# Causal masks and output scaling moved to VectorE, rotary products spread over three steps, in a transformer layer on eight cores

## The chip, the cores and the metric

The kernel runs on the 8 cores of one Trainium2 chip, one batch row each, with no exchange between them. The metric is device time in microseconds (us) of the slowest core. Engines are named as in the profile: PE is TensorE, DVE VectorE, ACT ScalarE, POOL GpSimd, and SP issues most transfers.

## The reference

One layer: a layer norm, causal attention with rotary positions in 16 heads of 64, and a feed-forward block with dequantized weights whose SiLU multiplies the attention output.

```python
xn = _layernorm(x)
q, k = rope(xn @ Wq), rope(xn @ Wk); v = xn @ Wv
attn = softmax(where(causal, q @ k.T / 8, -inf)); s = (attn @ v) @ Wo
h = layernorm(xn)
y = silu(h @ dequant(fc1) + b1); z = y @ dequant(fc2) + b2
x = x + s * silu(xn + 0.5 * z)
```

Each core has 2048 rows of 1024; the feed-forward width is 4096.

## The kernel before, in words

The program is written out in Python as one list of instructions for each engine; each engine works through its list in order, and semaphores hold it where it needs another's result. A core goes through four stages.

1. Rows are normalized and transposed, the first head pair is projected, and a quarter of the values (to about 112 us).
2. Attention. Heads are taken in pairs, `m` = 0 to 7. A pair has four groups of 512 queries, `qg`, and a group 2 `qg` + 2 steps `c` of two key tiles (128 keys each), so 20 steps for a pair and 160 in all. A step has the two tiles' `scores` (4 matmuls into `ps[0]` and `ps[1]`, then ACT's exponential to one of six buffers `pbuf`), filler matmuls, and then the `values` of the step before (8 matmuls that add into `ps[2]`: the weighted values in its first bank, the sum of weights in its second). Fillers are the projections of later pairs (`unit`, 8 matmuls, 8 units of work) and of the values (`v_unit`). They stand in one list and are handed out in proportion by `fill_to`, some 3.7 units of a matmul each in a middle step and 8.4 in a group's second, until step 133. From there, in the last part of pair 6 and pair 7, there are none ("the last head" below). A filler unit fills one of the two banks of `ps[3]`; DVE copies it out (L337 for queries and keys, L376 for values), and the unit after next waits for that copy (`f_free`).
3. `fc1`, 1024 matmuls with SiLU on ACT (620 to 850 us).
4. `fc2` and the output projection (850 us to the end).

What else stands in the attention steps: once a pair's queries or keys (`j` = 0, 1) are complete, SP issues four transfers that swap rows (`swp<-raw`), and three steps later `rope` has DVE multiply `swp` by the sine, `raw` by the cosine, and add both, each over 2048 columns. `later(n, fn)` puts work off by n steps, `step()` runs what is due. The sum is held back until the first step of the pair before, since it overwrites what the pair before that one read. 64 jobs (`dq_load`, `dq_do`) dequantize weights on DVE and write them to memory, 0.42 a step. On the two diagonal steps of each group (`c` = 2 `qg` and 2 `qg` + 1) the exponentials of a tile are multiplied by a mask (128 x 2 x 128) on POOL. At a group's end ACT takes logarithm and exponential of the weight sums (`linv`), DVE copies the weighted values out of their bank (`sol`), and POOL multiplies the two into `o_fm`. In the last head DVE also scales the activations for the next stage (`make_h`).

## Time and profile before

| | |
|---|---|
| median of 3 runs | 1144.39 us (1143.58 to 1147.31) |
| the profiled execution's own time | 1140.83 us |
| its span, slowest core (core 2) | 1139.3 us |
| spans of the other cores | 1124.7 to 1138.8 us |
| PE busy | 975.2 us (86%) |
| ACT busy | 475.6 us (42%) |
| DVE busy | 421.2 us (37%) |
| POOL busy | 181.2 us (16%) |
| PE's share of the chain that ended last | 70% |

A busy share is a mean over stages with different limits, so the stages are read apart. An engine's idle time is put down to what it waited for last; idle time of an engine that is not the limit costs nothing. The granted clock is TensorE's, as a share of 2.4 GHz.

### The profile page before, as it was taken

Reading aid. Unit: us, or ns where it says so; the run is one execution under the profiler, and the core shown is the slowest. Engines: PE = TensorE matmul, PEld = TensorE weight load, DVE = VectorE, ACT = ScalarE, POOL = GpSimd, SP = SyncE. Lnnn points to the kernel's source line nnn. Section 1 sums busy time; section 2 is a strip of 40 time slices with the busy share of each in tenths; the row PEclk is TensorE's granted clock in tenths of the full one; section 3 lists DMA queues with packets and bytes.
Section 4 is the critical chain, followed back from the end, with each engine's and each line's share of the span. In section 5 each row is a group of like instructions: output and inputs, shape, how many; then the busy total and the mean of one; then the engine's idle time right before and its main releaser. Section 6 shows DMA issues by size and latency. Waiting matters only on the chain.

```text
span 1139.3 us, 15271 instructions; the slowest of 8 cores (1124.7 to 1139.3 us)
## 1 busy us (share of the span) xinstructions
PE 975.2 (86%) x5465; PEld 423.5 (37%) x5465; DVE 421.2 (37%) x516; ACT 475.6 (42%) x616; POOL 181.2 (16%) x202
## 2 busy tenths in 40 slices
PE   3654588888788978799767999999997999999998
PEld 2332332332234322353223344444443444444443
DVE  3562454655564474546554000000002333333233
ACT  2232265656666765587888333333330000000000
POOL 1001031414243341425254000000000000000000
PEclk9767898989999998999889999999998999999999
DMA  7256457656586666457763855555547432234121
GB/s 186 75 169 102 102 187 237 174 196 195 158 248 201 206 187 203 158 186 245 239 184 100 184 152 157 154 155 157 150 111 267 139 139 83 112 139 144 50 65 37
DMA packets 92745, 180.47 MB, mean 158 GB/s; under 512 B 8048, under 2 KB 45056, under 8 KB 91392
## 3 DMA queue, kind: packets, MB, share of 16 engines
q1 hardware_dynamic: 84624, 170.52, 47.3%
q0 software_dynamic: 8048, 8.98, 5.5%
q8 instruction: 46, 0.75, 0.3%
q14 instruction: 27, 0.22, 0.1%
HBM read 138.11 MB, written 41.95 MB: 158 GB/s over the span
## 4 chain that ended last, share of the span: by engine, by line
PE 70%; DMA 8%; DVE 8%; issue 6%; ACT 5%; POOL 1%; SPq 1%; DVEq 0%; ACTq 0%; POOLq 0%
PE ps L860 20%; PE ps L793 18%; PE ps L328 8%; PE ps L664 8%; PE ps L367 5%; PE ps L625 5%; PE ps L835 4%; ACT pb L639 3%; DMA swp<-raw 3%; DMA y_spill<-yst 2%; DMA xbuf<-x 2%; DVE raw L337 1%; DVE raw L444 1%; POOL pb L645 1%; DVE swp L443 1%
## 5 line engine op out<-in xcount | busy, mean ns | idle before, releaser
L639 ACT ACTIVATE pb<-ps,negub 128x1024 bf16<-128x1024 f32 (+1 forms) x320 | 296.3, 981 | 148.4 <-PE ps L625 147.8
L793 PE MATMUL ps<-xn,w1t 128*128 128x512 bf16 x1024 | 224.0, 382 | 2.6 <-ACT yst L804 2.6
L328 PE MATMUL ps<-xn,wqk 128*128 128x512 bf16 x512 | 143.2, 404 | 40.0 <-DVE raw L337 33.9
L645 POOL TENSOR_TENSOR pb<-pb,msk 128x256 bf16<-128x256 bf16 x128 | 116.8, 928 | 266.3 <-ACT pb L639 263.8
L793 PEld LDWEIGHTS ps<-xn,w1t 128*128 128x128 bf16 x1024 | 100.7, 98 | 125.5 <-issue 8.3
L804 ACT ACTIVATE yst<-ps,b 128x512 bf16<-128x512 f32 x128 | 87.5, 687 | 136.3 <-PE ps L793 128.2
L875 ACT ACTIVATE tf<-tf 128x512 f32<-128x512 f32 x32 | 20.1, 630 | 267.3 <-DVE tf L871 267.3
L860 PE MATMUL ps<-w2a,ybuf 128*128 128x512 bf16 x512 | 118.3, 385 | 6.7 <-DMA ybuf<-y_spill 6.7
L860 PE MATMUL ps<-w2b,ybuf 128*128 128x512 bf16 x512 | 115.7, 379 | 0.0
L625 PE MATMUL ps<-qk,qk 64*128 64x512 bf16 (+3 forms) x640 | 101.4, 367 | 12.3 <-ACT pb L639 11.3
L664 PE MATMUL ps<-pb,v_tm 128*64 128x512 bf16 (+3 forms) x640 | 98.3, 378 | 13.7 <-POOL pb L645 11.7
L367 PE MATMUL ps<-wv,xn 128*128 128x256 bf16 x512 | 74.6, 295 | 41.2 <-DVE v_tm L376 29.1
L852 DVE TENSOR_SCALAR tf<-xt,mv,r 128x1024 f32<-128x1024 f32 x16 | 12.9, 809 | 241.5 <-DMA xt<-x 241.5
L664 PE MATMUL ps<-pb,ones 128*64 128x512 bf16 (+3 forms) x640 | 91.7, 367 | 0.0
L601 DVE SCALAR_TENSOR_TENSOR dqo<-dqi,dqs 128x1024 bf16<-128x1024 int32 x64 | 86.3, 1348 | 7.0 <-DMA dqs<-fc_scales 6.8
L328 PEld LDWEIGHTS ps<-xn,wqk 128*128 128x128 bf16 x512 | 43.0, 101 | 113.6 <-issue 84.4
L337 DVE CAST raw<-ps 128x512 bf16<-128x512 f32 x64 | 43.9, 688 | 111.1 <-PE ps L328 110.9
L860 PEld LDWEIGHTS ps<-w2a,ybuf 128*128 128x128 bf16 x512 | 50.6, 99 | 69.2 <-issue 10.5
L871 DVE SCALAR_TENSOR_TENSOR tf<-ps,tf 128x512 f32<-128x512 f32 x32 | 22.1, 691 | 145.0 <-PE ps L860 145.0
L367 PEld LDWEIGHTS ps<-wv,xn 128*128 128x128 bf16 x512 | 49.7, 105 | 66.9 <-issue 58.4
L860 PEld LDWEIGHTS ps<-w2b,ybuf 128*128 128x128 bf16 x512 | 50.1, 98 | 60.4
L625 PEld LDWEIGHTS ps<-qk,qk 64*128 64x128 bf16 x640 | 27.8, 94 | 87.7 <-issue 81.1
(74 smaller groups left out, 603.7 us busy)
## 6 DMA issues: line engine op xcount, KB each, us to landing
dqi<-fc_q SPq DMA_DIRECT2D x64, 512.0 KB, 4.7
dqs<-fc_scales SPq DMA_DIRECT2D x64, 512.0 KB, 6.1
w_deq<-dqo SPq DMA_DIRECT2D x64, 256.0 KB, 2.5
y_spill<-yst SPq DMA_DIRECT2D x32, 512.0 KB, 3.7
ybuf<-y_spill SPq DMA_DIRECT2D x8, 2048.0 KB, 10.0
xbuf<-x SPq DMA_DIRECT2D x16, 512.0 KB, 5.2
swp<-raw SPq DMA_DIRECT2D x64, 128.0 KB, 5.0
w1t<-w_deq SPq DMA_DIRECT2D x32, 256.0 KB, 4.2
```

The source lines that it names most:

```text
L328: fn = (lambda e: e.matmul(p, w[:, 128 * fc:128 * (fc + 1)], xn[:, S * fc + 512 * tg:S * fc + 512 * (tg + 1)], start=(fc == 0), stop=(fc = ...
L337: t_raw[(m, j, tg)] = VE.tick(lambda e: e.tensor_copy(raw[j][:, 512 * tg:512 * (tg + 1)], p))
L367: fn = (lambda e: e.matmul(z[:, 256 * u:256 * (u + 1)], xn[:, S * fc + 128 * t:S * fc + 128 * (t + 1)], wv[p][:, 256 * fc:256 * (fc + 1)], ...
L601: t_dv[k] = VE.tick(lambda e: e.scalar_tensor_tensor(dqo[k % 2][:], dqi[k % 2][:], -128.0, dqs[k % 2][:], ALU.add, ALU.mult))
L625: fn = (lambda jj, r: lambda e: e.matmul(z[:, 512 * jj + off:512 * (jj + 1)], ka[r:r + 64, 128 * kt:128 * (kt + 1)], qa[r:r + 64, 512 * qg ...
L639: tok = SC.tick(lambda e: e.activation(fap(p, [[512, 2], [1, n]], offset=off), fap(z, [[512, 2], [1, n]], offset=off), AF.Exp, bias=negub[ ...
L645: tok = GP.tick(lambda e: e.tensor_mul(fap(p, [[512, 2], [1, 128]], offset=off), fap(p, [[512, 2], [1, 128]], offset=off), fap(msk, [[0, 2 ...
L664: fn = (lambda what, jj, kt, p, off, w: lambda e: e.matmul(ps[2][64 * jj:64 * (jj + 1), 512 * what + off:512 * (what + 1)], w, p[:, 512 * ...
L793: fn = (lambda k, fc, f, tg: lambda e: e.matmul(ring[k], w1t[f % 4][:, 128 * fc:128 * (fc + 1)], xn[:, S * fc + 512 * tg:S * fc + 512 * (t ...
L804: t_ring[k] = SC.tick((lambda k, f, tg: lambda e: e.activation(yst[f % 2][:, 512 * tg:512 * (tg + 1)], ring[k], AF.Silu, bias=b1[:, f:f + ...
L835: fn = (lambda hf, fc: lambda e: e.matmul(z[:, 512 * hf:512 * (hf + 1)], o_fm[:, S * fc + 128 * t:S * fc + 128 * (t + 1)], wo[:, 1024 * fc ...
L860: fn = (lambda f, wt, lo, hi: lambda e: e.matmul(z[:, lo:hi], ybuf[i][:, 256 * f + 128 * (t % 2):256 * f + 128 * (t % 2) + 128], wt[:, 102 ...
```

## The change

Four things are moved, and none is computed in another way.

- The masks are multiplied on DVE instead of POOL, at the start of the next step (`mask`).
- The weighted values are multiplied by `linv` on DVE straight from their PSUM bank (`scale`), at the start of the next step; the copy to `sol` and POOL's product are gone.
- When a new group begins (`c` == 0), the values of the last step of the group before stand ahead of the fillers, not behind them.
- `rope` has its first product three steps after the unit, as before, the second a step later, and the sum a step after that, or at the first step of the pair before. In a step where such work is due no dequantization is written, unless more than two are owed; these are caught up afterwards. Ahead of the first step six calls of `step()` take the place of three.

```diff
@@ -157,8 +157,7 @@
     swp = [at(f"swp{j}", S, BF16, RE + 8192 + 4096 * j) for j in range(2)]
     sq = at("sq", S, BF16, RE + 16384)
     pbuf = [at(f"pb{i}", 1024, BF16, RF + 2048 * i) for i in range(6)]
-    sol = [at(f"sol{i}", 512, F32, RG + 2048 * i) for i in range(2)]
-    linv = [at(f"linv{i}", 512, F32, RG + 4096 + 2048 * i) for i in range(2)]
+    linv = [at(f"linv{i}", 512, F32, RG + 2048 * i) for i in range(2)]
     wqk = [[at(f"wqk{i}{j}", 1024, BF16, RH + 4096 * i + 2048 * j) for j in range(2)] for i in range(2)]
     cos_t = at("cos_t", S, BF16, RI)
     sin_t = at("sin_t", S, BF16, RI + 4096)
@@ -439,19 +439,22 @@
             f_free[b] = t_neg[m]
 
         def rope(m, j):
-            VE.wait(t_swap[(m, j)], t_cos)
-            VE.do(lambda e: e.tensor_mul(swp[j][:], swp[j][:], sin_t[:]))
-            tok = VE.tick(lambda e: e.tensor_mul(raw[j][:], raw[j][:], cos_t[:]))
-
-            def add():
+
+            def by_sin():
+                VE.wait(t_swap[(m, j)], t_cos)
+                VE.do(lambda e: e.tensor_mul(swp[j][:], swp[j][:], sin_t[:]))
+
+            def by_cos():
+                tok = VE.tick(lambda e: e.tensor_mul(raw[j][:], raw[j][:], cos_t[:]))
+
+                later(max(1, 7 + 20 * (m - 1) - now[0]), lambda: add(tok))
+
+            def add(tok):
                 VE.wait(tok, t_last_s.get(m - 2))
                 t_rope[(m, j)] = VE.tick(lambda e: e.tensor_add(qb[m % 2][j][:], raw[j][:], swp[j][:]))
 
-
-            if now[0] >= 4 + 20 * (m - 1):
-                add()
-            else:
-                later(4 + 20 * (m - 1) - now[0], add)
+            by_sin()
+            later(1, by_cos)
 
 
         for t in range(1, 4):
@@ -573,8 +576,8 @@
 
         total = sum(c for c, _ in fill)
         lead = 33.0
-        fill_to(12.0)
-        for _ in range(3):
+        fill_to(15.0)
+        for _ in range(6):
             step()
         fill_to(lead)
 
@@ -640,12 +644,16 @@
                 fap(p, [[512, 2], [1, n]], offset=off), fap(z, [[512, 2], [1, n]], offset=off),
                 AF.Exp, bias=negub[:, m:m + 1], scale=0.125))
             t_exp_bank[half] = tok
-            if kt >= 4 * qg:
-                GP.wait(tok, t_msk)
-                tok = GP.tick(lambda e: e.tensor_mul(
-                    fap(p, [[512, 2], [1, 128]], offset=off), fap(p, [[512, 2], [1, 128]], offset=off),
-                    fap(msk, [[0, 2], [1, 128]])))
             t_p[(m, qg, kt)] = tok
+
+        def mask(m, qg, kt):
+
+            off = 128 * (kt - 4 * qg)
+            p = pbuf[slot_of[(m, qg, kt)]]
+            VE.wait(t_p[(m, qg, kt)], t_msk)
+            t_p[(m, qg, kt)] = VE.tick(lambda e: e.tensor_mul(
+                fap(p, [[512, 2], [1, 128]], offset=off), fap(p, [[512, 2], [1, 128]], offset=off),
+                fap(msk, [[0, 2], [1, 128]])))
 
         def values(m, qg, c):
 
@@ -682,13 +690,16 @@
             t_bank[1] = SC.tick(lambda e: e.activation(linv[i][:], ps[2][:, 512:1024], AF.Ln))
             SC.wait(t_bank[1])
             t_li = SC.tick(lambda e: e.activation(linv[i][:], linv[i][:], AF.Exp, scale=-1.0))
-            VE.wait(tok, t_o.get(g - 2))
-            t_bank[0] = VE.tick(lambda e: e.tensor_copy(sol[i][:], ps[2][:, 0:512]))
-            GP.wait(t_li, t_bank[0])
-            if m >= 4:
-                GP.wait(t_vmm[m - 4])
-            t_o[g] = GP.tick(lambda e: e.tensor_mul(
-                o_fm[:, S * m + 512 * qg:S * m + 512 * (qg + 1)], sol[i][:], linv[i][:]))
+
+            def scale():
+                VE.wait(t_li)
+                if m >= 4:
+                    VE.wait(t_vmm[m - 4])
+                t_o[g] = VE.tick(lambda e: e.tensor_mul(
+                    o_fm[:, S * m + 512 * qg:S * m + 512 * (qg + 1)], ps[2][:, 0:512], linv[i][:]))
+                t_bank[0] = t_o[g]
+
+            at_next.append(scale)
 
 
         kinds = []
@@ -732,19 +743,27 @@
         prev = None
         ns = len(kinds)
         for s, (m, qg, c, w) in enumerate(kinds):
-            step()
+            ran = step()
+            for fn in at_next:
+                fn()
+            at_next.clear()
+            if prev and prev[2] >= 2 * prev[1]:
+                for kt in (2 * prev[2], 2 * prev[2] + 1):
+                    mask(prev[0], prev[1], kt)
             for kt in (2 * c, 2 * c + 1):
                 scores(m, qg, kt)
+            if c == 0 and prev:
+                values(*prev)
             if s < last_fill:
                 run += w
                 fill_to(lead + (total - lead) * run / weight)
             else:
                 fill_to(1e9)
-            if prev:
+            if c > 0:
                 values(*prev)
             prev = (m, qg, c)
             want = min(len(jobs), (len(jobs) * (s + 1)) // (ns - 8))
-            while done < want:
+            while done < want and (not ran or want - done > 2):
                 dq_do(done)
                 if done + 2 < len(jobs):
                     dq_load(done + 2)
@@ -757,7 +776,16 @@
                 for f in range(3):
                     load_w1(f)
         step()
+        for kt in (2 * prev[2], 2 * prev[2] + 1):
+            mask(prev[0], prev[1], kt)
         values(*prev)
+        for fn in at_next:
+            fn()
+        while done < len(jobs):
+            dq_do(done)
+            if done + 2 < len(jobs):
+                dq_load(done + 2)
+            done += 1
         t_att = (PE.sem, PE.n)
         while put_off:
             step()
```

How this moves instructions is seen at two places. The first is on DVE in the middle of pair 1, where the keys of pair 2 (`raw_73`, `swp_75`) get their rotary products while the second quarter of the values is projected (L376 copies a finished filler unit). Before:

```order
L418 TENSOR_REDUCE nm_62<-ps 1x2
L422 TENSOR_SCALAR nm_62<-nm_62 1x1
L430 TENSOR_SCALAR stb<-nm_62 1x1
L601 SCALAR_TENSOR_TENSOR dqo_98<-dqi_94,dqs_96 128x1024
L443 TENSOR_TENSOR swp_75<-swp_75,sin_t 128x2048
L444 TENSOR_TENSOR raw_73<-raw_73,cos_t 128x2048
L448 TENSOR_TENSOR qk_69<-raw_73,swp_75 128x2048
L376 CAST v_tm<-ps 128x2x256
L438 COPY negub<-ps 128x1
L601 SCALAR_TENSOR_TENSOR dqo_97<-dqi_93,dqs_95 128x1024
```

Now (DVE's rotary lines are L445, L448 and L454 here, and the dequantization is L604):

```order
L418 TENSOR_REDUCE nm_62<-ps 1x2
L422 TENSOR_SCALAR nm_62<-nm_62 1x1
L430 TENSOR_SCALAR stb<-nm_62 1x1
L604 SCALAR_TENSOR_TENSOR dqo_96<-dqi_92,dqs_94 128x1024
L445 TENSOR_TENSOR swp_75<-swp_75,sin_t 128x2048
L376 CAST v_tm<-ps 128x2x256
L448 TENSOR_TENSOR raw_73<-raw_73,cos_t 128x2048
L438 COPY negub<-ps 128x1
L454 TENSOR_TENSOR qk_69<-raw_73,swp_75 128x2048
L654 TENSOR_TENSOR pb_77<-pb_77,msk 128x2x128
L654 TENSOR_TENSOR pb_78<-pb_78,msk 128x2x128
```

The copy of the filler unit stood behind all three rotary operations and now stands behind the first; the second and the sum follow it, and two masks (L654) stand behind the sum.

The second place is on PE where pair 2 begins after the last group of pair 1. L625 (L629 now) is scores, L328 filler, L664 (L672 now) values, with `v_tm` for the weighted values and `ones` for the sums. Before:

```order
L664 MATMUL ps<-pb_81,ones_50 64x512 x2
L664 MATMUL ps<-pb_82,ones_50 64x384 x2
L625 MATMUL ps<-qk_68,qk_69 128x512 x2
L625 MATMUL ps<-qk_68,qk_69 128x384 x2
L328 MATMUL ps<-xn,wqk_89 128x512 x4
L328 MATMUL ps<-xn,wqk_90 128x512
L664 MATMUL ps<-pb_77,v_tm 64x256 x2
L664 MATMUL ps<-pb_78,v_tm 64x128 x2
L664 MATMUL ps<-pb_77,ones_50 64x256 x2
```

Now:

```order
L672 MATMUL ps<-pb_81,ones_50 64x512 x2
L672 MATMUL ps<-pb_82,ones_50 64x384 x2
L629 MATMUL ps<-qk_68,qk_69 128x512 x2
L629 MATMUL ps<-qk_68,qk_69 128x384 x2
L672 MATMUL ps<-pb_77,v_tm 64x256 x2
L672 MATMUL ps<-pb_78,v_tm 64x128 x2
L672 MATMUL ps<-pb_77,ones_50 64x256 x2
L672 MATMUL ps<-pb_78,ones_50 64x128 x2
L328 MATMUL ps<-xn,wqk_87 128x512 x4
```

The values of the finished group (`pb_77`, `pb_78`) stood behind the new group's scores and five filler matmuls; they now come right behind the scores.

## Rows read from the trace of the kernel before

**Rows 1.** Stretches, core 2: busy us of PE, PEld, DVE, ACT, POOL; clock, DMA, GB/s.

```profile
112.00:130.00 18.00, 7.26 (x47) 4.67 (x43) 10.08 (x14) 1.78 (x3) 0.00 (x0) 0.70 0.46 58
130.00:545.00 415.00, 354.11 (x2399) 138.59 (x2399) 222.82 (x249) 271.25 (x323) 135.91 (x140) 0.95 0.64 197
545.00:620.00 75.00, 54.34 (x379) 19.06 (x379) 40.13 (x39) 62.10 (x74) 30.76 (x30) 0.91 0.61 188
620.00:850.00 230.00, 226.29 (x1040) 101.86 (x1041) 0.69 (x1) 90.02 (x131) 5.59 (x10) 0.99 0.56 150
```

**Rows 2.** PE's waits while fillers last, 130 to 545 us: us, times, longest.

```profile
PE ps L328 <- DVE raw L337: 33.9, 17, 4.9
PE ps L367 <- DVE v_tm L376: 18.6, 8, 5.3
PE ps L664 <- POOL pb L645: 4.2, 9, 1.2
PE ps L625 <- ACT pb L639: 1.3, 4, 0.6
PE ps L328 <- DVE v_tm L376: 1.1, 1, 1.1
```

**Rows 3.** PE's waits in the last head, 545 to 620 us.

```profile
PE ps L664 <- POOL pb L645: 7.1, 10, 1.2
```

**Rows 4.** PE's timeline, nine of its long waits: start, us, [idle before, releaser].

```profile
163.90 0.59 PE L328 MATMUL ps<-xn,wqk 128*128 128x512 bf16 x1 [2.23 <-DVE raw L337]
...
185.69 1.86 PE L328 MATMUL ps<-xn,wqk 128*128 128x512 bf16 x4 [4.12 <-DVE raw L337]
...
233.24 1.01 PE L367 MATMUL ps<-wv,xn 128*128 128x256 bf16 x4 [5.28 <-DVE v_tm L376]
...
279.15 0.38 PE L328 MATMUL ps<-xn,wqk 128*128 128x512 bf16 x1 [3.16 <-DVE raw L337]
...
299.25 0.38 PE L328 MATMUL ps<-xn,wqk 128*128 128x512 bf16 x1 [4.01 <-DVE raw L337]
...
426.57 1.00 PE L328 MATMUL ps<-xn,wqk 128*128 128x512 bf16 x2 [3.17 <-DVE raw L337]
...
446.79 0.38 PE L328 MATMUL ps<-xn,wqk 128*128 128x512 bf16 x1 [4.86 <-DVE raw L337]
...
476.91 0.60 PE L367 MATMUL ps<-wv,xn 128*128 128x256 bf16 x4 [3.98 <-DVE v_tm L376]
...
529.40 0.81 PE L328 MATMUL ps<-xn,wqk 128*128 128x512 bf16 x3 [1.06 <-DVE raw L337]
```

**Rows 5.** DVE's timeline behind the wait that ends at 233.24 us.

```profile
227.66 1.23 DVE L601 SCALAR_TENSOR_TENSOR dqo<-dqi,dqs 128x1024 bf16<-128x1024 int32 x1
228.81 1.22 DVE L443 TENSOR_TENSOR swp<-swp,sin_t 128x2048 bf16<-128x2048 bf16 x1
229.94 1.22 DVE L444 TENSOR_TENSOR raw<-raw,cos_t 128x2048 bf16<-128x2048 bf16 x1
231.26 1.23 DVE L448 TENSOR_TENSOR qk<-raw,swp 128x2048 bf16<-128x2048 bf16 x1
232.41 0.69 DVE L376 CAST v_tm<-ps 128x512 bf16<-128x512 f32 x1
```

**Rows 6.** One stretch around that wait, columns as in rows 1.

```profile
232.10:238.90 6.80, 5.66 (x25) 2.06 (x25) 1.74 (x4) 1.91 (x2) 0.67 (x1) 0.50 0.27 92
```

**Rows 7.** Groups by line, whole span: count, busy us, mean ns, idle before.

```profile
L645 POOL TENSOR_TENSOR pb<-pb,msk 128x256 bf16<-128x256 bf16 x128 | 116.8, 928 | 266.3 <-ACT pb L639 263.8
...
L601 DVE SCALAR_TENSOR_TENSOR dqo<-dqi,dqs 128x1024 bf16<-128x1024 int32 x64 | 86.3, 1348 | 7.0 <-DMA dqs<-fc_scales 6.8
...
L686 DVE COPY sol<-ps 128x512 f32<-128x512 f32 x32 | 22.0, 688 | 44.4 <-PE ps L664 41.5 <-PE ps L625 1.5 <-POOL pb L645 1.2
...
L504 DVE TENSOR_TENSOR g2t<-g2t,mv 128x16 f32<-128x16 f32 x1 | 0.2, 175 | 0.1
```

**Rows 8.** DVE's waits for the swap transfer, 112 to 618 us.

```profile
DVE swp L443 <- DMA swp<-raw: 14.0, 5, 5.3
```

More of the change, by code:

```diff
@@ L229, in step @@
                 p[1]()
+            return len(due)
         t_c = None
@@ L608, in build_nc @@
         t_bank = [None, None]
+        at_next = []
         t_o = {}
```

## The prediction

> **What bounds the kernel now.** I read the profile in this order. First the table of stretches [rows 1]. The last two stages, from 620 us on, are untouched by the change, and TensorE (PE) is all but full there (226 of 230 us in the first of them). In the attention stage PE is busy for 354 of 415 us while filler matmuls last (130 to 545 us) and for 54 of 75 us in the last head, where there are none. ScalarE (ACT) is busy 271 of 415 us and 62 of 75 us. So with fillers PE sets the pace and ACT is starved by it; in the last head ACT is near its limit.
>
> Then PE's waits [rows 2]. With fillers PE loses 33.9 + 18.6 + 1.1 = 53.6 us to DVE's copies out of the two filler banks (L337, L376), 4.2 us to masks on POOL, 1.3 us to ACT. In the last head it loses 7.1 us to masks [rows 3]. Then PE's long waits in order of time [rows 4]. Of the 26 waits for those copies 15 take 1.06 us or more: the row at 163.90 is the first, that at 529.40 the last. Seven are longer than 2.46 us: 4.12, 5.28, 3.16, 4.01, 3.17, 4.86 and 3.98, together 28.6 us. The other eight (2.23, 2.08, 1.68, 1.86, 2.26, 1.40, 1.67, 1.06) make 14.2 us, the fifteen 42.8. The other eleven are the wait for a copy that has just begun.
>
> What is late is seen on DVE in one of them [rows 5]. PE wants the bank at 227.96. DVE, which works in the order of its program, has a dequantization (from 227.66), the three rotary operations (228.81, 229.94, 231.26) and only then the copy (232.41). From the first product's end to the copy there are 232.41 − 229.94 = 2.47 us, which the second product and the sum fill; so it is in the other windows too.
>
> After such a wait PE is slow: in the 6.8 us around that one the granted clock is 0.50, the lower level of 1.2 GHz [rows 6]. Over the 415 us it is 0.95 [rows 1], so 2 × 0.05 × 415 = 41 us ran at the lower level and cost half, 20 us. These 41 us lie in ten spans, each beside one of the waits of 1.86 us or more, 11 in all; the one of 2.08 us has none.
>
> **The change part by part.**
>
> *Rotary products over three steps.* Nothing is removed; the second product comes a step after the first, the sum a step after that or later, and a filler copy that is written between goes ahead of them. That is what the first pair of listings shows, at this very wait: the copy passes two of three operations. The wait there would be 5.28 − 2.46 = 2.8 us. Taking 2.46 us from each of the fifteen leaves 28.6 − 7 × 2.46 = 11.4 us in the seven long ones and nothing in the eight, a gain of 42.8 − 11.4 = 31.4 us. Not every one will find its copy between two pieces, and the shortest waits keep the length of their own copy (0.69 us [rows 5]), so I take 28 us. The bounds are 53.6 us (every wait for DVE goes) and 0 (the copy always lands outside the split).
> The dequantizations are held out of the steps that run a rotary piece; before, seven steps held a whole rotary group and one of 1.23 us. That is inside these 28 us. They are caught up two at a time in nine steps, 2.5 us in one piece. With the two banks, PE stops for that only where a copy is due within it.
> At the start (112 to 130 us) all six rotary pieces still stand in one piece without a filler between them: PE has 7.3 us busy in those 18 us [rows 1], and I count nothing there. Six steps in place of three move nothing on the engines by themselves.
>
> *The clock.* Of eleven waits of 1.86 us or more, two are left by the sum above (2.8 and 2.4 us). I leave three to be safe: 8 of 11 of the 20 us is 14.5, and I take 13 us. Bounds: 0 and 20.
>
> *Masks from POOL to DVE, a step later.* 128 operations of 928 ns leave POOL [rows 7]. What PE waits for them is 4.2 us with fillers and 7.1 us in the last head [rows 2, 3], 11.3 in all; I take 9 us. On DVE no row shows this form. The nearest are a two-input product of bfloat16, 2048 elements in 1.22 us [rows 5], and one of 16 float32 elements in 0.175 us [rows 7]. Between them lies 0.51 ns an element, so 0.175 + 256 × 0.51 = 0.31 us; at the float32 price (0.69 us for 512 elements [rows 7], 1.04 ns) it is 0.44 us. I take 0.31, the nearest row being the one of the same type: 104 masks in 415 us are 32 us of DVE. Against this DVE gets time back from POOL: a dequantization takes 1348 ns in the mean and 1.23 us where POOL is quiet [rows 5, 7], some 7 us over the 64, and the rotary products gain too. DVE's 223 us of 415 would become some 240, and it is not the bound.
> The row shows operations of DVE stretched when POOL runs. The Trainium skill ("SBUF — State Buffer", "SBUF: two separate sides") says why: VectorE with two SBUF inputs and GpSimd take one pair of ports in turns, and the loser is blocked for the whole instruction. By it a blocked operation would wait for a POOL mask's full 0.93 us, and the gain here would be some 7 us of DVE time either way; the sum does not change.
>
> *What the masks add to DVE's queue.* This is the price. A mask stands behind the copies and the dequantization of the step before, and PE's value products wait for it. For the first diagonal step of a group, from the timeline: values come some 0.8 us after the exponentials of that step end, masks need 0.6 us, so a copy and a dequantization just ahead make PE wait some 0.8 us. A filler unit ends in that step 0.44 of the time and 0.42 dequantizations fall on a step: 26 groups × 0.18 × 0.8 = 4 us. For the last step, whose values now stand ahead of the fillers, 26 × 0.11 × 1.1 = 3 us. A rotary piece of 1.22 us stands ahead in some 3 of 10 of these 52 steps and costs half a us: 8 us. Sum 15 us, of which I take 14. Bounds: 0 (PE always later), and 26 × 1.5 = 39 us if every group end waits for a piece of work and the masks. In the last head DVE also scales the activations for the next stage there, two operations of 1.22 and 0.97 us every second step, but PE has slack against ACT.
>
> *Values scaled from their bank.* The copy of 688 ns and POOL's product of some 1.4 us become one product from PSUM, by the nearest row 688 ns [rows 7]: nothing added. The accumulator's first bank is now free after ACT's two operations and this product, some 1.4 us later than by the copy. With fillers the next group's values stand behind a step's scores and 8.4 units of filler; that covers it. Without fillers the wait is 1 us, four times, beside ACT, which is the limit there: nothing. The second pair of listings shows the last values of a group ahead of the fillers. ACT takes the exponentials of the new group first in either order, so its logarithm starts when it did, and I count nothing for the move.
>
> **Sum.** −28 − 13 − 9 + 14 = −36 us. The profiled execution took 1140.8 us, and so 1104.8; the median shown, 1144.4, is 3.6 us above it, so I forecast 1108.
>
> **The rivals.**
> *More goes than I count.* If PE's waits for DVE fall to the 10.8 us of the eleven short ones, the clock stays up (−20) and the masks cost 5 us: −42.8 − 20 − 11.3 + 5 = −69 against 1144.4, and with a few left over some 1084. For it: DVE is free for 190 of 415 us. Against: three of the long waits also hold a wait for the swap transfer.
> *The waits only move.* The first product still waits three steps after the transfer is issued; DVE stood idle 14.0 us for it, five times, up to 5.3 us [rows 8]. Where it does, copies, masks and the scaling now all stand behind. If the masks' price is half as much again for that (+21) and the rotary term and the clock's give half (−14 − 7, with −9 for POOL), the sum is −9, so 1135.
> *No change* within 0.3%, about 3.4 us, which is what a measurement of this kernel can tell: the same, with the gain and price equal.
> *Slower.* DVE becomes the serial hub: every group's values wait for exponential, DVE's queue and mask. If each of the 32 group ends and of the 32 steps before it waited 1.5 us where none was before, that is 96 us; the gain of 50 us is used up at 0.8 us each, and at 1 us the time is 1144 + 64 − 50 = 1158. The rows speak against it: masks need two short operations, and DVE is idle for nearly half of the stage. The Trainium skill ("TensorE: Matmul & The Clock Gate", "Architectural detail") calls VectorE's queue strictly first in, first out, and so does the order in [rows 5]; that is what this rival needs.
> *The change doesn't do what it says* is excluded: the listings show it.
>
> **How the numbers follow.** Forecast (own range 1092 to 1122): 0.60. More: 0.14. Waits only move: 0.12. No change: 0.05. Slower: 0.09. Faster by over 0.3% is 0.60 + 0.14 + 0.12 = 0.86. The range for 8 in 10 leaves out the slow case, no change and half of "more": 1082 to 1136.
>
> **What would show it.** Right: PE's waits for L337 and L376 between start and last filler fall from 53.6 to some 25 us, the clock there rises to 0.98, waits for POOL are gone, DVE's masks take some 0.3 us, the stage up to 620 us ends some 36 us sooner, and the stages behind keep their length. Wrong: value products (L672) that wait for masks by more than 20 us in all; swap waits on DVE well over 14 us; long waits for L337 that keep their 4 to 5 us.

## The result: slower, where faster was forecast

The changed kernel takes 1156.09 us (median of 6 runs), the kernel before, run beside it, 1144.28 us (6 runs). The ratio is 1.0078, with a 95% interval of 1.004 to 1.0115. In two of the six runs of the changed kernel (1218.12 and 1289.81 us) one half of the chip had a lower granted clock; the median holds them, the ratio leaves them out. Forecast were 1108 us and a range of 1082 to 1136. The profiled run took 1154.38 us, its span is 1152.8 us, on core 1. The first matmul of the stage behind attention starts at 634.19 us; before it started at 620.50 us. What follows it lasts 518.6 us, before 518.8 us. So all that is lost is lost by the end of attention.

Here are the same stretches of the changed kernel as in [rows 1], with the same columns (busy us of PE, PEld, DVE, ACT and POOL, then clock, DMA share and GB/s):

```profile
112.00:130.00 18.00, 6.94 (x45) 4.53 (x44) 9.76 (x13) 1.78 (x3) 0.00 (x0) 0.72 0.38 48
130.00:545.00 415.00, 348.13 (x2348) 135.71 (x2345) 223.97 (x346) 264.09 (x315) 5.38 (x10) 0.94 0.64 193
545.00:620.00 75.00, 51.42 (x348) 18.50 (x349) 42.41 (x62) 57.72 (x70) 0.53 (x1) 0.84 0.71 209
```

PE does 6 us less in the 415 us than before and 3 us less in the 75 us, at a lower clock in both. POOL is all but empty, and DVE's sum is what it was (224 against 223 us): it took the masks in, its dequantizations are shorter (1219 ns in the mean, 1348 before), and less of its other work falls into these 415 us, since everything is later.

The next view holds the waits of the changed kernel between 112 and 640 us (us in total, times, longest), those of PE for DVE and those of DVE for transfers (six rows of the view; those of PE for ACT and of DVE for other engines are left out):

```profile
DVE dqo L604 <- DMA dqs<-fc_scales: 43.3, 15, 7.4
PE ps L328 <- DVE raw L337: 30.9, 14, 7.7
PE ps L672 <- DVE pb L654: 27.1, 22, 4.7
PE ps L367 <- DVE v_tm L376: 24.1, 10, 9.2
DVE swp L445 <- DMA swp<-raw: 15.1, 4, 5.5
PE ps L672 <- DVE o_fm L698: 6.6, 4, 1.7
```

The first row was not in the forecast. Before, DVE waited 6.8 us, three times, for the scales of a dequantization; now it waits 43.3 us, fifteen times. The copies of the filler units (L337, L376) are waited for nearly as long as before, with a longest wait of 7.7 us where [rows 2] have 4.9 (the 9.2 us row lies ahead of 130 us; before it was 9.6). The waits for masks are 27.1 us, where POOL's were 11.7.

DVE's timeline of the changed kernel shows one of the fifteen (start, us, operation, in brackets the idle time before it and its releaser):

```profile
438.53 2.35 DVE L604 SCALAR_TENSOR_TENSOR dqo<-dqi,dqs 128x1024 bf16<-128x1024 int32 x2
447.79 1.23 DVE L604 SCALAR_TENSOR_TENSOR dqo<-dqi,dqs 128x1024 bf16<-128x1024 int32 x1 [6.91 <-DMA dqs<-fc_scales]
448.93 0.68 DVE L408 TENSOR_REDUCE nm<-ps 128x1 f32<-128x512 f32 x1
449.53 1.21 DVE L445 TENSOR_TENSOR swp<-swp,sin_t 128x2048 bf16<-128x2048 bf16 x1
450.67 0.68 DVE L337 CAST raw<-ps 128x512 bf16<-128x512 f32 x1
```

and SP's, of the same place, when the loads were sent:

```profile
440.38 0.45 SPq L60 DMA_DIRECT2D dqi<-fc_q  x1
440.88 0.45 SPq L60 DMA_DIRECT2D dqs<-fc_scales  x1
...
441.92 0.43 SPq L60 DMA_DIRECT2D dqi<-fc_q  x1
442.39 0.93 SPq L60 DMA_DIRECT2D dqs<-fc_scales  x1
```

and PE's:

```profile
451.49 1.44 PE L328 MATMUL ps<-xn,wqk 128*128 128x512 bf16 x3 [7.69 <-DVE raw L337]
```

This reads as follows. Dequantizations held back during the rotary steps are caught up two in one piece at 438.53; this happens ten times in the changed kernel and never in the one before. A pair empties both input buffers. Each load goes out behind the dequantization that freed its buffer, the first at 440.38 and 440.88 (codes and scales), the second at 441.92 and 442.39; the next dequantization stands ready in DVE's queue and waits 6.9 us for the first of them. Behind it stand the reduction, the rotary product and, at 450.67, the copy that PE needs: PE stands for 7.7 us. The load is not an unusual one: it takes about the median from issue to landing, 6.9 us for scales (6.1 us before). What was lost is mostly the start ahead of time.

In the last head, where masks and scaling stand behind such a wait, it reads so (DVE, same columns):

```profile
563.45 2.47 DVE L604 SCALAR_TENSOR_TENSOR dqo<-dqi,dqs 128x1024 bf16<-128x1024 int32 x2
573.31 1.23 DVE L604 SCALAR_TENSOR_TENSOR dqo<-dqi,dqs 128x1024 bf16<-128x1024 int32 x1 [7.39 <-DMA dqs<-fc_scales]
576.52 1.23 DVE L604 SCALAR_TENSOR_TENSOR dqo<-dqi,dqs 128x1024 bf16<-128x1024 int32 x1 [1.98 <-DMA dqs<-fc_scales]
577.66 1.00 DVE L654 TENSOR_TENSOR pb<-pb,msk 128x256 bf16<-128x256 bf16 x4
584.38 1.22 DVE L604 SCALAR_TENSOR_TENSOR dqo<-dqi,dqs 128x1024 bf16<-128x1024 int32 x1 [5.72 <-DMA dqs<-fc_scales]
585.52 0.68 DVE L698 TENSOR_TENSOR o_fm<-ps,linv 128x512 bf16<-128x512 f32 x1
586.13 0.89 DVE L654 TENSOR_TENSOR pb<-pb,msk 128x256 bf16<-128x256 bf16 x4
```

One pair has three waits behind it, 15.1 us in all. The scaling and the masks at 585.52 and 586.13 came right behind the last, and PE waited 4.7 us for those masks, with no filler to do.

### The profile page after: what moved, and what is told of

It is laid out like the page before. It is cut to its first block, busy times and chain, and to the rows that moved or that the text cites. A ratio compares the mean times of both kernels' runs of the same rounds, so it can differ in the third digit from the quotient of the medians.

```text
span 1152.8 us, 15075 instructions; the slowest of 8 cores (1128.3 to 1152.8 us)
## 1 busy us (share of the span) xinstructions
PE 976.0 (85%) x5465; PEld 423.8 (37%) x5465; DVE 429.5 (37%) x644; ACT 475.8 (41%) x616; POOL 19.1 (2%) x42
## 2 busy tenths in 40 slices
DMA packets 92744, 180.47 MB, mean 157 GB/s; under 512 B 8048, under 2 KB 45056, under 8 KB 91392
## 4 chain that ended last, share of the span: by engine, by line
PE 70%; DMA 10%; DVE 8%; issue 6%; ACT 5%; SPq 1%; DVEq 0%; ACTq 0%; POOL 0%; POOLq 0%
PE ps L888 19%; PE ps L821 18%; PE ps L672 9%; PE ps L328 9%; PE ps L367 5%; PE ps L629 5%; PE ps L863 4%; DMA dqs<-fc_scales 4%; ACT pb L643 2%; DMA y_spill<-yst 2%; DVE dqo L604 1%; DMA xbuf<-x 1%; DVE raw L337 1%; DMA swp<-raw 1%; DMA wv<-wv 1%
## 5 line engine op out<-in xcount | busy, mean ns | idle before, releaser
L328 PE MATMUL ps<-xn,wqk 128*128 128x512 bf16 x512 | 143.6, 406 | 37.1 <-DVE raw L337 30.9
L903 ACT ACTIVATE tf<-tf 128x512 f32<-128x512 f32 x32 | 20.1, 629 | 267.5 <-DVE tf L899 267.5
L672 PE MATMUL ps<-pb,v_tm 128*64 128x512 bf16 (+3 forms) x640 | 97.7, 381 | 34.1 <-DVE pb L654 27.1
L629 PE MATMUL ps<-qk,qk 64*128 64x512 bf16 (+3 forms) x640 | 101.4, 372 | 11.9 <-ACT pb L643 10.8
L672 PE MATMUL ps<-pb,ones 128*64 128x512 bf16 (+3 forms) x640 | 93.5, 372 | 0.0
L604 DVE SCALAR_TENSOR_TENSOR dqo<-dqi,dqs 128x1024 bf16<-128x1024 int32 x64 | 77.2, 1219 | 43.4 <-DMA dqs<-fc_scales 43.3
L328 PEld LDWEIGHTS ps<-xn,wqk 128*128 128x128 bf16 x512 | 43.4, 101 | 107.4 <-issue 76.3
L337 DVE CAST raw<-ps 128x512 bf16<-128x512 f32 x64 | 44.1, 689 | 93.6 <-PE ps L328 93.5
L672 PEld LDWEIGHTS ps<-pb,v_tm 128*64 128x64 bf16 x640 | 27.9, 111 | 96.3 <-issue 94.3
L629 PEld LDWEIGHTS ps<-qk,qk 64*128 64x128 bf16 x640 | 26.1, 95 | 90.5 <-issue 88.0
```

Source lines behind the costliest of these rows:

```text
L328: fn = (lambda e: e.matmul(p, w[:, 128 * fc:128 * (fc + 1)], xn[:, S * fc + 512 * tg:S * fc + 512 * (tg + 1)], start=(fc == 0), stop=(fc = ...
L337: t_raw[(m, j, tg)] = VE.tick(lambda e: e.tensor_copy(raw[j][:, 512 * tg:512 * (tg + 1)], p))
L604: t_dv[k] = VE.tick(lambda e: e.scalar_tensor_tensor(dqo[k % 2][:], dqi[k % 2][:], -128.0, dqs[k % 2][:], ALU.add, ALU.mult))
L629: fn = (lambda jj, r: lambda e: e.matmul(z[:, 512 * jj + off:512 * (jj + 1)], ka[r:r + 64, 128 * kt:128 * (kt + 1)], qa[r:r + 64, 512 * qg ...
L672: fn = (lambda what, jj, kt, p, off, w: lambda e: e.matmul(ps[2][64 * jj:64 * (jj + 1), 512 * what + off:512 * (what + 1)], w, p[:, 512 * ...
```

## The experiments

The theory (H) from these rows: the holding back of dequantizations ("the hold" below), to which the prediction gave no price of its own, is what turns the gain into a loss, by way of the input buffers. Its rivals: the masks and the scaling on DVE cost it (M), the last values ahead of the fillers cost it (V), or the split of the rotary products gives nothing (R). Each run has the ratio of its time to that of the kernel before on the same chip, with its 95% interval.

**Without the hold.** The changed kernel, each step with its due dequantizations:

```diff
-            while done < want and (not ran or want - done > 2):
+            while done < want:
```

> The changed kernel with its dequantizations written where they were before, also in steps that run rotary work. Theory H (holding them back is the fault: two are then done at once, both buffers are loaded in one round, and DVE stands before the next one): DVE's waits for the loads fall from 43.3 us to under 12, PE's waits for masks from 27.1 us to under 15, its waits for filler copies from 56 to under 45, and the time to 1120 to 1135 us. Theory M (the masks and the scaling in DVE's queue are the fault, whatever the loads do): PE's waits for masks stay above 20 us and the time stays at 1145 to 1158 us.

Measured: 1130.64 us, ratio 0.9878 (0.9859 to 0.9898). That is 2.0% less than with the hold, and faster than before. Its waits between 112 and 640 us:

```profile
PE ps L672 <- DVE pb L654: 22.2, 22, 2.0
PE ps L367 <- DVE v_tm L376: 21.6, 9, 9.2
PE ps L328 <- DVE raw L337: 21.3, 15, 5.6
DVE swp L445 <- DMA swp<-raw: 10.1, 6, 5.0
DVE dqo L604 <- DMA dqs<-fc_scales: 9.1, 2, 6.9
PE ps L672 <- DVE o_fm L698: 6.3, 4, 1.6
```

Time, waits for scales (43.3 to 9.1 us) and waits for copies are as H expects; PE's for L337 fall from 30.9 to 21.3. The waits for masks miss it: 22.2 us, where H expected under 15. They have another cause.

**The hold alone**, put into the kernel before, whose rotary group stays whole (`step()` also returns how many pieces it ran, as in the changed kernel, and what is owed at the end is caught up there):

```diff
-            step()
+            ran = step()
...
-            while done < want:
+            while done < want and (not ran or want - done > 2):
```

> The kernel before with one part of the change: dequantizations are held out of steps with rotary work and caught up later; masks, scaling, rotary products and values as before. Theory H: DVE's waits for the loads rise from 6.8 us to over 20, and the time is 1148 to 1158 us. Theory M: the loads' waits are covered or small, and the time is 1138 to 1147 us.

Measured: 1144.56 us, ratio 0.9996 (0.9976 to 1.0015). That is M's range; H expected 1148 to 1158 us, and this expectation failed, though the waits for scales rise as it said, to 20.1 us, nine times, against 6.8 before. The traces show a difference to the changed kernel: here no two dequantizations stand in one piece, where the changed kernel has ten such pairs, and only 7.7 of the 20.1 us fall between 130 and 545 us, where fillers last (25.5 of 43.3 in the changed kernel). So the hold costs by what it meets in the changed kernel.

**A third pair of input buffers** in the changed kernel, hold and all; a load then goes out three dequantizations ahead (the third load at the start and the semaphore slots that go with it are left out here):

```diff
-    dqi = [at(f"dqi{i}", 1024, I32, RK + 4096 * i) for i in range(2)]
-    dqs = [at(f"dqs{i}", 1024, F32, RK + 8192 + 4096 * i) for i in range(2)]
+    dqi = [at(f"dqi{i}", 1024, I32, RK + 4096 * i if i < 2 else RG + 4096) for i in range(3)]
+    dqs = [at(f"dqs{i}", 1024, F32, RK + 8192 + 4096 * i if i < 2 else RG + 8192) for i in range(3)]
...
-                if done + 2 < len(jobs):
-                    dq_load(done + 2)
+                if done + 3 < len(jobs):
+                    dq_load(done + 3)
```

> The changed kernel, dequantizations held back as it does, but with three pairs of input buffers for them, so that a load is issued three jobs ahead and not two. Theory H: DVE's waits for the loads fall from 43.3 us to under 10, and the time to 1120 to 1135 us, as in the run without holding back. If it is not the loads but the double dequantization itself (2.4 us in one piece) that costs: the loads' waits fall, but the time stays above 1145 us. Theory M: 1145 to 1158 us too, with PE's waits for masks above 20 us.

Measured: 1133.63 us, ratio 0.9897 (0.9876 to 0.9918). Here the hold stays and only the loads are early, and the time is that without the hold (the intervals overlap). No wait for scales is left; one for the store of a dequantized tile takes its place (w_deq, 10.8 us, five times). The ten pairs are still there. So the hold's price goes through the empty input buffers, and no price of the 2.5 us that a pair takes is seen beyond the intervals (the two ratios are 0.2% apart).

**The split alone**, in the kernel before: `rope` as in the change's diff, and six calls of `step()` ahead of the first step.

```diff
-            VE.wait(t_swap[(m, j)], t_cos)
-            VE.do(lambda e: e.tensor_mul(swp[j][:], swp[j][:], sin_t[:]))
-            tok = VE.tick(lambda e: e.tensor_mul(raw[j][:], raw[j][:], cos_t[:]))
...
+            by_sin()
+            later(1, by_cos)
...
-        for _ in range(3):
+        for _ in range(6):
             step()
```

> The kernel before with one part of the change: the rotary products over three steps; dequantizations where they were. The prediction's step (2.46 us off each long wait): PE's waits for filler copies between 130 and 545 us fall from 53.6 to 25 to 32 us, the time to 1105 to 1118 us. The rival that the waits only move: they fall by less than 12 us and the time stays above 1134 us.

Measured: 1123.5 us, ratio 0.9801 (0.9782 to 0.982). R falls: the split gives 2.0%, some 23 us. The time lies above the 1105 to 1118 us of the prediction's step and below the 1134 us of the rival that the waits only move: neither expectation came. PE's waits for DVE's copies while fillers last (130 to 545 us) are these:

```profile
PE ps L328 <- DVE raw L337: 23.1, 14, 6.4
PE ps L367 <- DVE v_tm L376: 13.9, 9, 2.8
```

37.0 us of the 53.6 in [rows 2] stay, where the prediction expected some 25. DVE's timeline at one of the long ones that are left (PE stands until 435.67, 3.77 us):

```profile
433.70 1.22 DVE L445 TENSOR_TENSOR swp<-swp,sin_t 128x2048 bf16<-128x2048 bf16 x1 [3.15 <-DMA swp<-raw]
434.84 0.68 DVE L337 CAST raw<-ps 128x512 bf16<-128x512 f32 x1
435.44 1.21 DVE L448 TENSOR_TENSOR raw<-raw,cos_t 128x2048 bf16<-128x2048 bf16 x1
```

The split works as listed: the copy stands between the first and the second product. But the first product waits for its swap transfer, which SP sent from 425.68 on, and the copy waits with it.

**Split and masks on DVE**, without the rest (hunks of the change for `mask`):

```diff
-            if kt >= 4 * qg:
-                GP.wait(tok, t_msk)
...
+            if prev and prev[2] >= 2 * prev[1]:
+                for kt in (2 * prev[2], 2 * prev[2] + 1):
+                    mask(prev[0], prev[1], kt)
```

> The kernel before with the rotary products split (1123.5 us by itself) and the masks on DVE a step later; scaling, order of the values and dequantizations as before. If the masks on DVE are what cost the 7 us that lie between that run and the one without holding back: 1128 to 1133 us, with PE waiting over 15 us for masks. If it is the order of the values: 1118 to 1125 us, with PE's waits for masks under 10 us, since a filler stands between a group's last scores and its values.

Measured: 1124.63 us, ratio 0.9819 (0.9786 to 0.9852), against 0.9801 for the split alone: no difference that the intervals tell apart. The time is that of the second expectation, the waits are not: PE waits 19.1 us for masks (13 times), where under 10 were expected and the split alone has 13.2 us for POOL's. The longest, 6.2 us at 574.84, has four masks behind a normalization on DVE that waited 4.95 us for its weights. Waits for ACT are the same (12.4 and 12.5).

**Split and scaling on DVE**, masks on POOL:

```diff
-            VE.wait(tok, t_o.get(g - 2))
-            t_bank[0] = VE.tick(lambda e: e.tensor_copy(sol[i][:], ps[2][:, 0:512]))
...
+            at_next.append(scale)
```

> The kernel before with the rotary products split and the values scaled on DVE from their bank; masks on POOL, order of the values and dequantizations as before. By the prediction's count (the scaling costs nothing): within 2 us of 1123.5 us. If the accumulator's bank, free later, costs: some 1.6 us of PE's wait for it at each group end without fillers and where DVE stands before ACT's reciprocal with copies behind it, 1126 to 1130 us.

Measured: 1134.73 us, ratio 0.9908 (0.9876 to 0.9939), so 1.1% over the split alone and more than either expectation. PE waits for the scaling 17.5 us, eleven times. The longest, on PE and then on DVE:

```profile
576.30 1.06 PE L668 MATMUL ps<-pb,v_tm 128*64 128x512 bf16 x4 [7.47 <-DVE o_fm L693]
```

```profile
573.41 1.22 DVE L717 TENSOR_TENSOR xn<-xn,g_rep 128x2048 bf16<-128x2048 bf16 x1 [7.85 <-DMA g_rep<-g_row]
574.75 0.81 DVE L719 TENSOR_SCALAR xn<-xn,gam,bet 128x2048 bf16<-128x2048 bf16 x1
575.48 0.68 DVE L693 TENSOR_TENSOR o_fm<-ps,linv 128x512 bf16<-128x512 f32 x1
```

The load of the second normalization's weights (g_rep) is issued by POOL, behind its masks; DVE waits 7.85 us for it with the scaling behind, and PE's bank is not free until then. With the masks gone from POOL, in the other kernels with `scale`, this wait for `g_rep` is not there. That it makes the whole 1.1% is not shown: the other ten waits for the scaling take 10.0 us together and none over 1.8, and the run with the masks on DVE had a wait of 6.2 us by the same load and lost no time that could be measured.

**Without hold, last values behind the fillers.** The kernel of the first experiment with the order of before:

```diff
-            if c == 0 and prev:
-                values(*prev)
...
-            if c > 0:
+            if prev:
                 values(*prev)
```

> The changed kernel without holding back (1130.6 us) and with a group's last values behind the fillers again; masks and scaling on DVE. If the order of the values is what makes PE wait for masks (in that run most of the waits stand before values of 256 columns, a group's last step): PE's waits for masks fall from 22.2 us to under 10 and the time to 1119 to 1125 us. If the masks are late for DVE's queue whatever the order: over 15 us of waits and 1128 to 1133 us.

Measured: 1125.0 us, ratio 0.9821 (0.9791 to 0.9851), 0.6% under the first experiment; the two intervals, from two chips, just stay apart. PE's waits for masks fall from 22.2 to 11.8 us. That is near the first expectation (1119 to 1125 us, under 10 us of waits), with the waits just over it, and far from the second. It is also the kernel with split, masks and scaling; it stands at the time of the split alone (0.9801, intervals overlap). So M falls where both are moved and nothing is held, within what the intervals can tell (0.3% or so).

**Split with a third pair of input buffers.** The edit is that of the third-pair experiment (at other addresses), on the kernel with the split alone.

> The kernel before with the rotary products split and a third pair of input buffers for the dequantizations. In the run with the split alone DVE waited 12.2 us for loads, most of it late, where masks and copies behind it have slack: the waits fall under 4 us and the time is 1118 to 1124 us. A gain over 6 us would say that the loads still set DVE's pace even with dequantizations spread evenly.

Measured: 1120.7 us, ratio 0.9798 (0.9766 to 0.9831), as expected. It does nothing there: 12.2 us of waits for scales are gone, and the swap waits are 20.1 us (13.7 without it), those for L337 26.9 (23.1).

**Split with the hold**, masks and scaling on POOL (the expectation has the scaling on ScalarE; ACT only makes `linv`):

```diff
-            while done < want:
+            while done < want and (not ran or want - done > 2):
```

> The kernel before with the rotary products over three steps (which alone gave 1123.5 us) and with the holding back of weight dequantizations, masks on GpSimd and scaling on ScalarE as before. Theory A, that the hold costs by the loads' waits alone (two dequantizations in one piece empty both input buffers, VectorE stands 7 us for the loads each time): at least 1138 us, VectorE's waits for scales and codes in 112:640 over 30 us. Rival B, that it costs only with masks and scaling behind it in VectorE's queue: 1120 to 1131 us, though the waits for scales rise.

Measured: 1135.26 us, ratio 0.9897 (0.9872 to 0.9923), between the two expectations and nearer to A: 1.0% over the split alone. DVE's waits between 112 and 640 us have this row:

```profile
DVE dqo L605 <- DMA dqs<-fc_scales: 53.7, 20, 7.7
```

There are again ten pairs. So the loads' waits cost with no mask or scaling behind them; with both and the early values the same hold costs 2.0%.

**Split with the last values ahead of the fillers**, masks on POOL:

```diff
+            if c == 0 and prev:
+                values(*prev)
             if s < last_fill:
...
-            if prev:
+            if c > 0:
                 values(*prev)
```

> The split alone (1123.5 us) with the last values of a group put ahead of the fillers, masks on GpSimd. Theory A, that the order costs by itself: TensorE reaches the last scores' masks too early whichever engine makes them, TensorE's waits for masks in 112:640 rise from 13.2 to over 22 us, 1128 to 1136 us. Rival B, that only masks on VectorE are late there: waits for masks under 17 us and at most 1126 us.

Measured: 1135.34 us, ratio 0.9897 (0.9872 to 0.9922), A. PE's waits of this kernel between 130 and 545 us:

```profile
PE ps L667 <- POOL pb L648: 25.2, 38, 1.4
PE ps L328 <- DVE raw L337: 15.6, 14, 2.8
PE ps L367 <- DVE v_tm L376: 12.4, 8, 2.8
```

Waits for masks are 25.2 us in place of 8.1, whichever engine makes them: PE comes to the values right behind the new group's scores, before the last exponentials have been masked. The waits for the copies fall by 9 us, and it costs 1.0% all the same.

**Split, third pair, and the rotary work four steps after the copy:**

```diff
-                    later(3, lambda: rope(m, j))
+                    later(4, lambda: rope(m, j))
```

> The split with a third pair of input buffers (1120.7 us) and the rotary work four steps after the copy, not three. Theory, that what stays of TensorE's waits for the copies comes from VectorE standing for the swap transfer: VectorE's swap waits in 112:640 fall from 20.1 to under 6 us, TensorE's waits for the copies (L338) from 26.9 to under 18, time 1108 to 1116 us. Rival, that the copies wait for the amount of work in VectorE's queue, wherever the swap stands: within 3 us of 1120.7, waits for the copies as before.

Measured: 1108.47 us, ratio 0.9658 (0.9633 to 0.9684), the theory's range, at its lower end. The waits for L337 (the expectation's L338) go from 26.9 to 12.5 us, with a longest one of 1.4, and DVE's for the swap from 20.1 to 7.6, where under 6 were expected.

**The same without the third pair.** The one-word edit on the kernel with the split alone.

> The kernel before with the rotary products split and done four steps after the copy, with the two pairs of input buffers of before (three steps after, it took 1123.5 us; with a third pair and four steps 1108.5 us). Theory A, that the step later is what gives and the third pair nearly nothing: ratio to before 0.966 to 0.971 (about 1107 to 1112 us), TensorE's waits for the copies in 130:545 under 15 us (23.1 at three steps). Rival B, that both are needed, since dequantizations that wait for their loads still stand ahead of the copies: ratio 0.973 to 0.979, waits for the copies over 18 us.

Measured: 1107.33 us, ratio 0.9673 (0.9651 to 0.9695): A. Its waits of PE from 130 to 545 us, and its stretch with fillers:

```profile
PE ps L367 <- DVE v_tm L376: 12.7, 9, 2.4
PE ps L328 <- DVE raw L337: 12.6, 13, 1.4
PE ps L667 <- POOL pb L648: 12.2, 21, 1.2
```

```profile
130.00:545.00 415.00, 366.29 (x2578) 146.38 (x2580) 240.46 (x266) 299.76 (x358) 160.31 (x155) 0.99 0.73 216
```

With the 1.1 us of a third row (L328 for the copy L376) the 53.6 us are 26.4 now, the clock is 0.99, and PE is busy 12 us more of the 415 than before the change. DVE's waits for the swap are 7.3 us, where the split alone had 13.7. It is the simplest of the kernels near 1108 us.

**All parts that did not cost, with both repairs** (split, masks and scaling on DVE, no hold, last values behind, third pair, four steps); of its edit against the changed kernel these two places:

```diff
-                    later(3, lambda: rope(m, j))
+                    later(4, lambda: rope(m, j))
...
-            while done < want and (not ran or want - done > 2):
+            while done < want:
```

> All parts of the change that did not cost by themselves, with the two repairs: masks and scaling on VectorE, rotary products split and one step later (four steps after the copy), no holding back, last values behind the fillers, a third pair of input buffers. Theory A, that masks and scaling on VectorE neither give nor cost once nothing long stands ahead of them: within 4 us of the same kernel with both left where they were (1108.5 us). Rival B, that they free time, since waits for masks fall from 15.9 to under 8 us: 1096 to 1103 us. Rival C, that they load VectorE's queue and the copies come late again: over 1114 us, waits for the copies over 20 us.

Measured: 1121.16 us. By the number alone that is rival C, but the kernel before took 1155.19 us on this chip, 9 to 11 us more than on the others, and its waits for L337 are 15.6 us, not over 20; the run has no ratio of its own and settles nothing. The same program on another chip:

> The same program as e12_all_later4, on another chip, beside e13. Theory A, that masks and scaling on VectorE neither give nor cost once nothing long stands ahead of them: ratio to before 0.963 to 0.969, as the kernel with a third pair and four steps (0.9658). Rival B, that they cost: ratio over 0.970. Rival C, that they give: under 0.962.

Measured: 1109.91 us, ratio 0.9695 (0.9677 to 0.9713), between A (up to 0.969) and B (over 0.970). Against the kernel without masks and scaling on DVE, run on the same chip (0.9673), the intervals overlap: the two moves give nothing, and whether they cost 0.2% stays open.

The parts, as ratios to before (each run beside the kernel before on its own chip; differences of 0.3% are within the intervals):

| kernel | ratio |
|---|---|
| split alone | 0.980 |
| + masks and scaling on DVE | 0.982 |
| + last values ahead of the fillers | 0.988 |
| + hold (the change) | 1.008 |
| split alone, work a step later | 0.967 |

## Why the prediction was wrong

**The step that failed** is this one: "The dequantizations are held out of the steps that run a rotary piece ... That is inside these 28 us. They are caught up two at a time in nine steps, 2.5 us in one piece. With the two banks, PE stops for that only where a copy is due within it." It counted DVE's 2.5 us and left out the transfers that a moved dequantization issues. With two pairs of buffers a load goes out behind each dequantization for the one after the next; two in one piece leave none under way long enough. What the runs showed in its place: waits for scales of 43.3 us and a price of 2.0% (1130.64 without the hold, 1133.63 with the hold and a third pair), some 23 us of the 48 us between forecast and result. [Rows 7] show 6.8 us of waits for scales already before. The rest, by ratios (9 us above before in place of 36 below, so 45 us to explain), is 18 us that the split did not give and some 7 us for the order of the values, less some 3 us by which masks and scaling cost less than forecast.

**Last values ahead of the fillers: "I count nothing for the move".** Wrong by 0.6% in this kernel and by 1.0% alone. ACT does take the new group's exponentials at once in either order, as was said; but the fillers between scores and values were also what covered the masks of the last step. The prediction did give these masks 3 us, for what stands in DVE's queue ahead of them; the waits for masks rose by 10.4 us (22.2 against 11.8).

**Rotary products over three steps: right in its mechanism, too large.** 28 us and 13 us for the clock were forecast, 23 us came. The copy lands between the pieces, and where nothing else is late the wait is as forecast: PE's wait at 233.50 us in the changed kernel is 2.86 us, forecast 2.8 for the one of 5.28. But 37.0 us of waits were left, not 25. At the place shown the reason is that the copy behind the first product inherits the product's wait for the swap transfer; [rows 8] had 14.0 us of such waits, and the prediction took them only into a rival. With the work a step later, 15 us more come (ratio 0.967 against 0.980), and waits and clock are close to what the prediction wanted of the split: 26.4 us and 0.99.

**Masks on DVE: about right in the sum.** Taken were 9 us of gain and 14 us of price. Without hold and early values PE waits 11.8 us for them, where POOL's cost 11.7, so what POOL's masks cost came back as waits for DVE's, and the time doesn't change beyond the intervals (0.982 and 0.980; +5 us were forecast, +2 came). One mask operation was put at 0.31 us and takes 0.286:

```profile
L604 DVE SCALAR_TENSOR_TENSOR dqo<-dqi,dqs 128x1024 bf16<-128x1024 int32 x64 | 77.2, 1219 | 43.4 <-DMA dqs<-fc_scales 43.3
...
L654 DVE TENSOR_TENSOR pb<-pb,msk 128x256 bf16<-128x256 bf16 x128 | 32.7, 286 | 22.6 <-ACT pb L643 21.9
...
L698 DVE TENSOR_TENSOR o_fm<-ps,linv 128x512 bf16<-128x512 f32 x32 | 22.0, 687 | 24.5 <-ACT linv L692 24.5
```

These are groups by line of the changed kernel (busy us, mean ns, idle before). The scaling from its bank takes 687 ns, as taken, and costs nothing that could be measured together with the masks. Alone it costs 1.1%, of which one wait of 7.5 us, by a load behind POOL's masks, is explained. That it stood next to a wait for a load was not seen.

**The rivals.** "The waits only move" named the right thing, a transfer with copies, masks and scaling behind it, but the wrong transfer, and gave 1135 us. "Slower" gave 1158 us, close to the 1156.09 measured, but by luck: it was a serial hub in which every group end waits, 64 times 1 us, and PE waited for masks and scaling 26 times, 33.7 us in all. The loss came from fifteen waits for loads and from the order of the values. Of the signs that the prediction listed for being wrong two came: value products that wait for masks by more than 20 us (27.1), and long waits for L337 (7.7).

**What stays open.** Why the hold costs nothing in the kernel before, though waits for scales rise there by 13 us, was not tried by itself. It fits that a whole rotary group holds for one step and not for three in a row, so that no two dequantizations fall together, and that most of those waits lie in the last head; that this is the cause is argued. The rest of the 1.1% of the scaling alone is open too. The waits of the values for masks (11.8 us) and of PE for short copies (26.4 us) were not taken further.

## What to carry to other kernels

When a step of a double-buffered load is postponed or bunched, price the transfers that it triggers: two in one piece emptied both buffers here, and the next one waited almost a whole landing time (6.9 us) with everything behind it. Before work is put into an in-order queue, look at which of its instructions wait for a transfer, and give those one more step first: here one step more gave 15 us, and was worth more than all that was moved off other engines. Matmuls that look like fillers in the way are often the cover of a chain on other engines; moving values ahead of them took that cover away.

## What the hardware showed beside it

With neither masks nor the scaling on POOL, DVE's dequantizations no longer stretch. This view gives the shortest, the median and the longest of the 64, before and then in the changed kernel:

```profile
L601 DVE SCALAR_TENSOR_TENSOR dqo<-dqi,dqs x64: 1207/1218/2144, 141.5 to 602.7; 128x1024 bf16<-128x1024 int32 x64
```

```profile
L604 DVE SCALAR_TENSOR_TENSOR dqo<-dqi,dqs x64: 1212/1217/1227, 139.6 to 614.0; 128x1024 bf16<-128x1024 int32 x64
```

The mean falls from 1348 to 1219 ns, 8 us over the 64; it is 1295 with the scaling alone on POOL (split and masks on DVE; the longest 2290 ns) and 1276 with the masks alone (split and scaling on DVE; the longest 1695 ns). The longest before stands beside POOL's scaling and not beside a mask, as POOL's and DVE's timelines show:

```profile
152.74 1.27 POOL L690 TENSOR_TENSOR o_fm<-sol,linv 128x512 bf16<-128x512 f32 x1 [2.39 <-ACT linv L684]
```

```profile
152.94 2.14 DVE L601 SCALAR_TENSOR_TENSOR dqo<-dqi,dqs 128x1024 bf16<-128x1024 int32 x1
```

It started 0.20 us after the product, which had 1.07 us to go, and took 0.92 us more than the median. Beside masks alone the longest took 0.48 us more than the median, so a wait of a mask's full 0.93 us, which the prediction names, was not seen there. The Trainium skill ("SBUF — State Buffer", "SBUF: two separate sides") says that of VectorE with two SBUF inputs and GpSimd the one that starts first has the shared ports for its whole instruction, and the other is blocked. The row at 152.94 agrees with that, nearly to the 1.07 us, and the 0.48 us don't speak against it, since who comes late waits only for what is left. Freed time on DVE gave nothing that the ratios show (0.982 against 0.980).

Transfers also landed later in the changed kernel, though it moves the same 180.47 MB: codes in 5.7 us in the median (4.7 before), scales in 6.9 (6.1), swaps in 5.7 (5.0). The runs tie this to the hold. Without it the changed kernel has 4.9, 6.1 and 4.6 us; with it the split goes from 5.1, 6.6 and 4.9 to 5.6, 7.5 and 5.7. That the loads of a pair share the queues with each other and with the stores would explain it, but was not tried by itself.
